# A graph kernel's preparation, rearranged: edge arrays in 112 rows, minima and maxima spread by TensorE, interleaved records, x loaded transposed

## The reference

```python
# layer 0: message network over edges, summed by destination
m = relu(concat([x[src], x[dst], e]) @ W1 + b1) @ W2 + b2;  x = norm(x + segment_sum(m, dst))
# layer 1: edge features
msg = relu(x[src] + edge_attr @ We + be);  h = (1 + eps) * x + segment_sum(msg, dst)
h = leaky(relu(h @ W1 + b1) @ W2 + b2);  x = norm(x + norm(h) * gamma + beta)
# layer 2: 3 rounds of x = A x with a degree-normalised weighted adjacency A, then a weighted mean
# layer 3: 10 rounds of h = 0.9 A' h + 0.1 x;  x = norm(x + h)
```

## Time and profile before

| | |
|---|---|
| median of 3 runs | 3042.13 us (3038.65 to 3044.47) |
| profiled execution | 3042.15 us, its span 3040.2 us |
| busy share of the span | TensorE 82%, VectorE 57%, GpSimd 44%, ScalarE 12% |
| chain that ended last | TensorE 55%, GpSimd 18%, issue 12%, DMA 5%, VectorE 4% |
| preparation | 0 to 110 us |
| layer 0, its norm, layer 1 | 110 to 1015, to 1057, to 1955 us |
| layers 2 and 3 | to 3040 us |

### The profile page before, as it was taken

One profiled execution on the slowest core, in us unless ns is written; L12 is line 12 of the kernel. 1 busy time (PEld: TensorE's weight loads), 2 busy tenths in 40 slices (PEclk: granted clock), 3 DMA queues, 4 the chain that ended last, 5 costly groups with the idle time before them and its releaser, 6 DMA issues.

```text
span 3040.2 us, 52876 instructions
## 1 busy us (share of the span) xinstructions
PE 2506.4 (82%) x16368; PEld 1680.1 (55%) x16368; DVE 1729.9 (57%) x3162; ACT 369.5 (12%) x840; POOL 1343.1 (44%) x1432
## 2 busy tenths in 40 slices
PE   2488888888888478888787888659979999999997
PEld 1377777777777366666666666533323333333332
DVE  2677777777776477778777777658531111111112
ACT  1011212111121011111111111110010000000000
POOL 0477777777777277777777777400000000000000
PEclk8699999999999599999999999869989999999998
DMA  1622222222222223222222222129988999999996
GB/s 38 80 53 52 53 52 53 51 53 58 60 53 51 32 50 79 65 64 66 63 66 63 65 65 64 47 88 342 362 286 281 352 347 340 340 337 336 346 349 219
DMA packets 410067, 442.29 MB, mean 145 GB/s; under 512 B 184975, under 2 KB 223861, under 8 KB 406788
## 3 DMA queue, kind: packets, MB, share of 16 engines
q1 hardware_dynamic: 354194, 367.83, 38.2%
q0 software_dynamic: 45248, 46.42, 7.9%
q10 hardware_dynamic: 10546, 26.89, 2.4%
HBM read 410.83 MB, written 30.14 MB: 145 GB/s over the span
## 4 chain that ended last, share of the span: by engine, by line
PE 55%; POOL 18%; issue 12%; DMA 5%; DVE 4%; ACT 3%; ACTq 1%; SPq 1%; POOLq 0%; DVEq 0%
PE bank L1438 28%; POOL arena L602 18%; PE bank L1309 8%; PE bank L1285 7%; PE bank L1297 5%; PE bank L1277 2%; ACT arena L1112 2%; PE bank L1413 2%; DMA arena<-in_edge_weight 2%; PE bank L1273 1%; PE bank L1442 1%; DMA arena<-d_p,arena 1%; DMA arena<-d_t,arena 1%; ACT arena L1122 1%; PE bank L1262 1%
## 5 line engine op out<-in xcount | busy, mean ns | idle before, releaser
L1438 PE MATMUL bank<-arena 128*64 128x512 f32 (+1 forms) x4368 | 895.3, 544 | 70.6 <-DVE arena L964 33.3
L602 POOL DMA_INDIRECT arena<-d_t,arena x707 | 667.0, 943 | 279.1 <-issue 218.6
L602 POOL DMA_INDIRECT arena<-d_p,arena x707 | 667.3, 944 | 255.5 <-issue 220.0
L1438 PEld LDWEIGHTS bank<-arena 128*64 128x64 f32 x4368 | 321.0, 136 | 557.4 <-issue 475.6
L1309 PE MATMUL bank<-arena 128*128 128x200 f32 x3136 | 565.3, 332 | 0.0
L1309 PEld LDWEIGHTS bank<-arena 128*128 128x128 f32 x3136 | 531.7, 190 | 7.9
L1285 PE MATMUL bank<-arena 128*128 128x320 bf16 x3030 | 479.1, 312 | 0.0
L1297 PE MATMUL bank<-arena 128*65 128x47 f32 x3232 | 240.0, 242 | 197.6 <-ACT arena L1112 187.8
L1285 PEld LDWEIGHTS bank<-arena 128*128 128x128 bf16 x3030 | 310.8, 103 | 141.3 <-issue 5.1
L1009 DVE TENSOR_TENSOR arena<-bank,arena 128x256 f32<-128x256 f32 (+1 forms) x70 | 27.8, 397 | 617.2 <-PE bank L1413 617.2
L759 DVE TENSOR_TENSOR arena<-arena,bank 128x1600 f32<-128x1600 f32 x196 | 356.8, 1820 | 6.8
(11 more groups left out here) (170 smaller groups left out, 1655.9 us busy)
## 6 DMA issues: line engine op xcount, KB each, us to landing
arena<-d_w SPq DMA_DIRECT2D x312, 1024.0 KB, 8.8
d_w<-arena ACTq DMA_DIRECT2D x24, 1024.0 KB
arena<-d_code SPq DMA_DIRECT2D x202, 64.0 KB
arena<-in_edge_attr SPq DMA_DIRECT2D x101, 128.0 KB
arena<-d_p,arena POOLq DMA_INDIRECT x707
arena<-d_t,arena POOLq DMA_INDIRECT x707
arena<-d_rec SPq DMA_DIRECT2D x392, 8.0 KB
arena<-in_src SPq DMA_DIRECT2D x202, 4.0 KB
```

Of the source, the lines that this page charges most:

```text
L602: g.indirect_dma_start(G[:, b, j, 0:F], None, table, bass.IndirectOffsetOnAxis(ap=idx[:, b, j:j + 1], axis=0)).then_inc(r.g[b], 16)
L1438: last = t.matmul(banks[t_ % 4][F * (n % 2):F * (n % 2) + F, 0:w_], old[:, n, :], right, start=n < 2, stop=False)
```

## The change

The constants: `NROW = 112` rows of 1024 (`EPL = 112 * 1024`), of which rows 102 to 112 hold padding. The host pads `src`, `dst`, `edge_weight`, `edge_weight1` to that and passes x also transposed.

- `dst`, `src`, `edge_weight` are loaded in 112 rows, `edge_weight1` in its first 101. Each has its own semaphore, and VectorE starts with `dst` alone.
- x transposed comes from DRAM; the transposes and copies go. x itself and `be` are loaded at the end of ScalarE's preparation.
- Minima and maxima are spread by products with ones and a diagonal, the row below by a shifted identity; `dst`, `edge_weight1` and the high codes by transposes out of the rows. The stores and reloads go, as do the loads by tile.
- VectorE computes the differences per row (`over`) and takes the flag from one transposed column. A window's first tile is the count of tiles whose maximum lies below it, one instruction per quarter.
- The records stay in row order, interleaved by VectorE and ScalarE in place; `d_rec` is flat, and the loop's record load takes 4 tiles with 32 runs of 4 edges each.
- The table's three casts move to ScalarE, the two subtractions stay on VectorE. In layer 1 the memsets come ahead of them.

The diff, cut to its core:

```diff
+NROW = 16 * -(-NSB // 16)
+EPL = NROW * SBE
...
-        d_rec = dram("d_rec", [P, NT, 4])
+        d_rec = dram("d_rec", [EPL, 4])
...
@@ block.sync
-            sp.dma_start(dstN, dst.rearrange("(p e) -> p e", e=SBE)).then_inc(s.ld_edges, 16)
-            sp.dma_start(srcN, src.rearrange("(p e) -> p e", e=SBE)).then_inc(s.ld_edges, 16)
-            sp.dma_start(fld[3], ew.rearrange("(p e) -> p e", e=SBE)).then_inc(s.ld_edges, 16)
-            sp.wait_ge(s.prep_v, 5)
-            sp.dma_start(d_tmin.rearrange("(p k) -> p k", k=8), tmin).then_inc(s.st_min, 16)
-            sp.dma_start(d_tmax.rearrange("(p k) -> p k", k=8), tmax).then_inc(s.st_min, 16)
-            sp.dma_start(d_bmin.rearrange("(p k) -> p k", k=1), bmin).then_inc(s.st_min, 16)
-            sp.wait_ge(s.st_min, 48)
-            sp.dma_start(bB, d_bmin.rearrange("(o k) -> o k", o=1).to_broadcast([P, NSB])).then_inc(s.ld_bc, 16)
-            sp.dma_start(tminB, d_tmin.rearrange("(o k) -> o k", o=1).to_broadcast([P, NT])).then_inc(s.ld_bc, 16)
-            sp.dma_start(tmaxB, d_tmax.rearrange("(o k) -> o k", o=1).to_broadcast([P, NT])).then_inc(s.ld_bc, 16)
-            sp.dma_start(dstS, dst.rearrange("(i p k) -> p i k", p=P, k=8)).then_inc(s.ld_sb, 16)
-            sp.dma_start(ewall, ew1.rearrange("(i p k) -> p i k", p=P, k=8)).then_inc(s.ld_sb, 16)
+            sp.dma_start(dstN, dst.rearrange("(p e) -> p e", e=SBE)).then_inc(s.ld_dst, 16)
+            sp.dma_start(srcN, src.rearrange("(p e) -> p e", e=SBE)).then_inc(s.ld_src, 16)
+            sp.dma_start(ewN, ew.rearrange("(p e) -> p e", e=SBE)).then_inc(s.ld_ew, 16)
+            sp.dma_start(ew1N, ew1.rearrange("(p e) -> p e", e=SBE)[0:NSB, :]).then_inc(s.ld_ew1, 16)
...
-            sp.wait_ge(s.rec_c, 8)
-            sp.dma_start(d_rec, rec).then_inc(s.st_rec, 16)
+            sp.wait_ge(s.prep_v, V_REC)
+            sp.wait_ge(s.rec_c, 1)
+            sp.dma_start(d_rec.rearrange("(p e) f -> p e f", e=SBE), rec).then_inc(s.st_rec, 16)
...
-                    sp.wait_ge(s.st_rows, 32)
+                    sp.wait_ge(s.prep_v, V_ROWS)
                     sp.wait_ge(s.st_rec, 16)
                     for w in range(2):
                         lo = sp.value_load(lo_row[0:1, ds(2 * k + w, 1)], min_val=0, max_val=NT - TPW)
                         if w == 0:
                             sp.wait_ge(s.pair_v[b], kh + 1)
                         sp.dma_start(wrec[:, b, w * TPW:(w + 1) * TPW, :],
-                                     d_rec[:, ds(lo, TPW), :]).then_inc(s.wrec[b], 16)
+                                     d_rec.rearrange("(t p k) f -> t p k f", p=P // TPW, k=TPW)[ds(lo, TPW), :, :, :].rearrange("t p k f -> (t p) k f")).then_inc(s.wrec[b], 16)
...
@@ block.vector
+            d.memset(w1ab[F:F + 1, :], 0.0).then_inc(s.clear, 1)
+            d.memset(w2p, 0.0).then_inc(s.clear, 1)
+            d.memset(xT[F:F + 1, :], 1.0).then_inc(s.clear, 1)
+            v.wait_ge(s.ld_dst, 16)
...
+            prep(d.tensor_copy(rec[:, :, 2], dstN))
+            dstF = rec[:, :, 2].rearrange("p (k e) -> p k e", e=P)
+            prep(d.tensor_reduce(tmin, dstF, AX, ALU.min))
+            prep(d.tensor_reduce(bmin, tmin, AX, ALU.min))
+            prep(d.tensor_reduce(tmax, dstF, AX, ALU.max))
             prep(d.tensor_scalar(tmax, tmax, float(N - 1), None, ALU.min))
-            prep(d.tensor_reduce(bmin, tmin, AX, ALU.min))
-            prep(d.tensor_scalar(srcI[0], srcN, P - 1, None, ALU.bitwise_and))
-            prep(d.tensor_scalar(srcI[1], srcN, 7, None, ALU.logical_shift_right))
-            prep(d.tensor_copy(fld[0], srcI[0]))
-            prep(d.tensor_copy(fld[1], srcI[1]))
-            assert V_IN[0] == V_FLD
-            prep(d.tensor_copy(srcT, srcN.rearrange("p (q k) -> p q k", k=8)[:, :, 7]))
+            v.wait_ge(s.ident, 3)
+            prep(d.tensor_scalar(bminD, ident[0:NSB, 0:NSB], bmin[0:NSB, :], None, ALU.mult))
+            assert V_IN[0] == V_BMIN
+            prep(d.tensor_tensor(tmaxD, tmax[0:NSB, :].unsqueeze(1).to_broadcast([NSB, NSB, 8]),
+                                 ident[0:NSB, 0:NSB].unsqueeze(2).to_broadcast([NSB, NSB, 8]), ALU.mult))
+            assert V_IN[0] == V_TMAX
+            v.wait_ge(s.ld_src, 16)
...
+            nxt = banks[4][0:NSB, 0:8]
+            hi_, lo_ = tmax[0:NSB, :], tmin[0:NSB, :]
+            v.wait_ge(s.bc_t, B_MIN)
+            d.scalar_tensor_tensor(over[:, 0:7], hi_[:, 0:7], 0.0, lo_[:, 1:8], ALU.add, ALU.subtract).then_inc(s.bad, 1)
+            d.scalar_tensor_tensor(over[:, 7:8], hi_[:, 7:8], 0.0, nxt[:, 0:1], ALU.add, ALU.subtract).then_inc(s.bad, 1)
+            d.scalar_tensor_tensor(over[:, 8:12], hi_[:, 0:4], float(WIN), lo_[:, 4:8], ALU.add, ALU.subtract).then_inc(s.bad, 1)
+            d.scalar_tensor_tensor(over[:, 12:16], hi_[:, 4:8], float(WIN), nxt[:, 0:4], ALU.add, ALU.subtract).then_inc(s.bad, 1)
+            d.scalar_tensor_tensor(over[:, 16:17], hi_[:, 7:8], float(1 - SPAN), bmin[0:NSB, :], ALU.add, ALU.subtract).then_inc(s.bad, 1)
+            v.wait_ge(s.bad, 5)
+            prep(d.tensor_reduce(over[:, 17:18], over[:, 0:17], AX, ALU.max))
+            assert V_IN[0] == V_WORST - 1 and V_CODE == V_WORST - 2
+            prep(d.tensor_copy(base_row, banks[4][0:1, 16:16 + NSB]))
+            prep(d.tensor_copy(bB, banks[4][:, 16:16 + NSB]))
+            v.wait_ge(s.bc_t, B_WORST)
+            prep(d.tensor_reduce(worst, banks[7][0:1, 0:NSB], AX, ALU.max))
+            d.tensor_scalar(flag, worst, 0.0, None, ALU.is_gt).then_inc(s.flag, 1)
             v.wait_ge(s.flag, 1)
...
+            prep(d.tensor_scalar(srcI[0], srcN, P - 1, None, ALU.bitwise_and))
+            prep(d.tensor_copy(rec[:, :, 0], srcI[0]))
+            prep(d.tensor_scalar(srcI[1], srcN, 7, None, ALU.logical_shift_right))
+            prep(d.tensor_copy(rec[:, :, 1], srcI[1]))
+            assert V_IN[0] == V_REC
+            v.wait_ge(s.bc_t, B_DST)
+            for half in range(2):
+                prep(d.tensor_tensor(rel.rearrange("p (i k) -> p k i", k=8)[:, 4 * half:4 * half + 4, :],
+                                     banks[half][:, 0:4 * NSB].rearrange("p (k i) -> p k i", i=NSB),
+                                     bB.unsqueeze(1).to_broadcast([P, 4, NSB]), ALU.subtract))
+            v.wait_ge(s.consts, C_ALL)
+            v.wait_ge(s.bc_c, 2)
             for q in range(4):
...
+                prep(d.tensor_scalar(below, tmaxB[0:WQ, :], edge8[:, q:q + 1], 0.0, ALU.is_lt, ALU.add, accum_out=lohi[:, q:q + 1]))
+            prep(d.tensor_scalar(lohi[:, 4:8], lohi[:, 0:4], float(NT - TPW), None, ALU.min))
+            assert V_IN[0] == V_LO
+            def halves(x_):
+                return x_.rearrange("p (r a) f -> p r a f", a=SLICES)
+            def part(z):
+                return X[:, :, z, :, :].rearrange("p a r f -> p r a f")
+            def rests(layer, whole, rest):
+                v.wait_ge(s.tab, 5 * layer + 1)
+                d.tensor_tensor(halves(rest), halves(whole), part(0), ALU.subtract).then_inc(s.tab, 1)
+                v.wait_ge(s.tab, 5 * layer + 3)
+                d.tensor_tensor(halves(rest), halves(rest), part(1), ALU.subtract).then_inc(s.tab, 1)
+            rests(0, PQ[:, :, 0:F], rest0)
...
+            v.wait_ge(s.ew_c, 2)
             by_order(v, general0, ordered0)
...
-            table(1, lnB, rest1)
             link(d.memset(aggT, 0.0))
             link(d.memset(WEBD, 0.0))
             assert cnt[0] == NB_WEBD
+            rests(1, lnB, rest1)
+            v.wait_ge(s.tab, 10)
...
@@ block.scalar
+            act.dma_start(xT[0:F, :], xt).then_inc(s.ld_xt, 16)
+            act.wait_ge(s.clear, 4)
+            act.dma_start(w1ab[0:F, 0:F], W1_0[0:F, :]).then_inc(s.ld_wts1, 16)
+            act.dma_start(w1ab[0:F, F:P], W1_0[F:2 * F, :]).then_inc(s.ld_wts1, 16)
+            act.dma_start(w1ab[F:F + 1, F:P], b1_0.rearrange("(o f) -> o f", o=1)).then_inc(s.ld_wts1, 16)
...
+            act.wait_ge(s.ld_ew, 16)
+            a.activation(rec[:, :, 3], ewN, ACT.Copy).then_inc(s.rec_c, 1)
+            def cast(z, from_):
+                a.activation(X[:, :, z, :, :].rearrange("p a r f -> p r a f"), from_.rearrange("p (r a) f -> p r a f", a=SLICES),
+                             ACT.Copy).then_inc(s.tab, 1)
+            act.wait_ge(s.pq_c, 7)
+            cast(0, PQ[:, :, 0:F])
+            act.wait_ge(s.bc_t, B_MAX)
+            for half in range(2):
+                a.activation(tmaxB[:, half * (NT // 2):half * (NT // 2) + NT // 2], banks[5 + half][:, 0:NT // 2], ACT.Copy).then_inc(s.bc_c, 1)
+            act.wait_ge(s.bc_t, B_EW)
+            for half in range(2):
+                a.activation(ewall.rearrange("p i k -> p k i")[:, 4 * half:4 * half + 4, :],
+                             banks[2 + half][:, 0:4 * NSB].rearrange("p (k i) -> p k i", i=NSB), ACT.Copy).then_inc(s.ew_c, 1)
+            act.wait_ge(s.bc_t, B_HI)
+            a.activation(hiS, banks[4][:, 0:NSB], ACT.Copy).then_inc(s.hi_c, 1)
```

(39 more changed lines are left out.)

211 lines of the change are left out of this document (65 added, 146 removed).

## The result

The changed kernel takes 2951.46 us (median of 4 runs, 2950.97 to 2953.62), the kernel before 3040.39 us beside it (4 runs). The ratio is 0.971, 95% interval 0.9693 to 0.9727: 89 us less, where 79 were forecast. The result lies only 0.5 us above the lower end of the forecast's range. The profiled execution took 2953.62 us, its span is 2951.8 us.

The account below looks back on a forecast made before the run. It took GpSimd's gathers to bound both message layers, so only earlier first gathers count: 69.7 us in layer 0 plus 9.3 in layer 1, 79.0 off 3042.15, gives 2963 us, range 2951 to 2982.

Parts of the forecast that it names:

- What bounds the kernel: Both message layers: 707 GpSimd gathers each, 1.25 us per gather; time before a layer's first gather counts one for one.
- Loads: Start of preparation: 112-row edge arrays spread over all engines; dst lands at 5 us, the rest by 9.
- P and Q: Node products in the preparation: x transposes and copies go; start 11.5 us, products 6.2 us, last copy 18.9.
- VectorE: VectorE's preparation work: flag at 25.1 us, records 28.9, counts 34.0, range rows 39.7, last table part 41.0.
- SyncE and the first gather: Layer 0's start: codes land about 35.5 us, first gather 5.1 later at 41 instead of 110.7; gain 69.7 us.
- new queue behind one engine: Rival, preparation: stores behind the 101-row load or ScalarE blocked behind x; first gather at 50, 2970 to 2984 us; chance 0.23.
- Does the layer follow: Layer 0's third superblock: first sums ready at 57.7 us, GpSimd asks at 58.5, so the layer follows its first gather.
- Layer 1: Between the layers: memsets ahead of the table bring layer 1's first gather 9.3 us earlier, at least 2.8.
- Records in the loops: Message loops: load of four tiles' records has some 6 us of cover, so it is priced at nothing.
- Between 1970 us and the end there is only dense work that the diff doesn't touch: Stretch after the message layers: taken as unchanged, with no gain or loss in the sum.
- more than counted: Rival, preparation: P/Q and VectorE overlap better, layer runs as if started at 34 to 36; 2955 to 2957 us; chance 0.17.

Follow-up runs that it names:

- e1: Changed kernel with 133 empty TensorE instructions that added nothing to the program, so a plain repeat of it; 2950.13 us.
- e6: Changed kernel with edge_weight1 also loaded as 112 rows instead of 101; ratio 0.9784 to the kernel before, at a lower TensorE clock.
- e9: Changed kernel with preparation reordered: broadcasts and dst transposes before node products, source columns written earlier, codes' store first; ratio 0.986 to the kernel before.
- e10: e9 with edge_weight1 also loaded as 112 rows; ratio 0.9831 to the kernel before, first gather at 41.77 us.
- e12: e10 with the record store moved to ScalarE's queue and x and its bias loaded after SyncE's layer 0 loop; 2945.57 us.
- e4: Changed kernel with the two memsets between layer 0 and layer 1 put back behind the table; 2960.85 us.
- e2: Kernel before with 123 empty TensorE instructions that added nothing to the program, so a plain repeat of it; 3041.3 us.
- e11: Changed kernel with 15 more matmuls (60 instructions) in TensorE's never-entered branch, shifting the product loop's code; ratio 0.9869 to the kernel before.

## Why the prediction came out as it did

- *What bounds the kernel*: right. Both loops follow their first gather to within 3 us (4.8 in e1), and the first gathers hold 77 of the 88 us. The sum for this part was 79.0; with the 3.3 us that the loops lost, 74 came of it.
- *Loads*: right in kind and a little early in size. dst landed at 4.8 us, edge_weight at 12.3; forecast 5 and 9.
- *P and Q*: the term of the preparation that was mis-sized most. Start 11.5 forecast, 14.35 measured (the bias row took 7.2 us, taken at 2.2); duration 6.2 forecast, 11.0 measured. Together they put VectorE's release at 26.2 us; it had waited 11.7.
- *VectorE*: the reductions over every fourth element took 1.95 us each (forecast 1.2), relative destinations 1.8 (1.0), counts 1.06 (0.95). Flag at 30.5 (25.1), ranges at 46.7 (39.7).
- *SyncE and the first gather*: 42.79 against 41, and by the forecast's path: the codes landed at 37.0 (35.5), the gather followed 5.8 us later (5.1). VectorE and TensorE were 5 to 7 us late, but it cost little here: the flag (30.5) came ahead of the codes' landing, and the first stores of P and Q, begun at 22.2 and not at 17, had been counted from 25. That the lateness fell where it was covered is luck. The loaded engine was met as forecast, Q's first store was held 4.9 us behind it (1.5 in e6); the rival "new queue behind one engine", first gather at 50, did not come. e9, e10 and e12 show that an earlier flag alone brings the gather little, since the record store's 1.8 MB comes next.
- *Does the layer follow*: it lost 3.0 us, 1.6 by one long gather of unknown cause and 1.1 by late indices of the second superblock, not by ScalarE's queue (the bias blocked it 3.03 us, forecast 2.3). But the sums of the first superblocks are as close as the forecast said: e1 and e4 lose 1.8 and 1.5 us more to them.
- *Layer 1*: 9.3 forecast, 9.3 measured (9.2 between the repeats e1 and e2), 9.2 in the trace when undone. Repeats of one kernel differ by 2.3 us in this stretch, so that the agreement to 0.1 us is in part luck.
- *Records in the loops*: nothing, as priced: from the fourth superblock to the last one, layer 0 takes 858.5 us before and 858.6 after, and layer 1 keeps its 892 us.
- *"Between 1970 us and the end there is only dense work that the diff doesn't touch"*: the step that failed, a term put at nothing. The diff doesn't touch that code, but it removes 61 instructions ahead of it, and there lay 12.5 of the 14.6 us. The forecast of 2963 is 11.5 us above the result, nearly all of it this. Had the changed loop fallen where before's did, as in e11, it would have come out near 2964, by these numbers. That the result lies in the range all the same is no merit of the reasons given for its lower end: the rival "more than counted" (2955 to 2957) spoke of the preparation, which gave less than the sum, not more.

## What to carry to other kernels

First look at how many rows a load has, before looking at how many bytes: 101 against 112 rows was worth 46 us of 3040 by itself. When a late, dense loop changes its period though no line in it was touched, read the instruction queue's packets before and inside the loop; a few dozen instructions that never run can switch it. And once a preparation is bound by the volume of its stores, order and queues give little: fewer bytes, not an earlier flag, would be the next thing to try (not tested here).
